# Gather stage of a two-layer graph kernel: four of a group's eight one-hot expansions moved from ScalarE to VectorE

## The reference

```python
weight = h @ (W_fc2 / 8.0)                # per edge, 4 x 32: wA, wC, wD, wB
g0, g1 = f0[edge_src], f1[edge_src]       # gathered rows, 32 and 32 x 3
e0, e1 = edge_attr[:, :1], edge_attr[:, 1:]
outA = wA * g0 * e0
outB = wB * einsum('euk,ek->eu', g1, e1) / SQRT3
outC = (wC * g0)[..., None] * e1[:, None, :]
outD = wD[..., None] * g1 * e0[..., None]
seg = lambda v: segment_sum(v, edge_dst)  # then scaled, mixed by small matrices, cos/sin, layernorm
```

## Time and profile before

| | us |
|---|---|
| median of 3 runs | 5282.36 (5281.97 to 5292.77) |
| the profiled execution | 5279.33 |
| its span, first to last instruction | 5277.7 |
| busy in the span: PE, VectorE, ScalarE, GpSimd | 3462.9, 2873.6, 2739.3, 4071.0 |
| gather stage, first to last gather instruction's start | 3262.97 to 5229.25 |

### The profile page before, as it was taken

How to read it: one execution, slowest core, us unless ns; L and a number is a source line. 1 busy time by engine, 2 the same in 40 slices (tenths; PEclk the granted TensorE clock), 3 DMA queues, 4 the chain that set the end, 5 groups by cost and what they waited for, 6 DMA issues and landing times. The chain is left out here.

```text
span 5277.7 us, 85398 instructions
## 1 busy us (share of the span) xinstructions
PE 3462.9 (66%) x18515; PEld 2879.1 (55%) x18515; DVE 2873.6 (54%) x12090; ACT 2739.3 (52%) x9367; POOL 4071.0 (77%) x3270
## 2 busy tenths in 40 slices
PE   3555555555555555555555376888888888888886
PEld 2334433344343443334333254878888888888886
DVE  5555556555556555565555366344454445444444
ACT  1222222222222222222222156899989998998997
POOL 2888888888888888888888764777777777777774
PEclk8777666666766666767676578777777777777777
DMA  8666666666666666666666595333333333333332
GB/s 278 114 114 109 117 110 114 114 115 113 108 114 114 115 115 113 111 110 115 115 114 113 82 245 153 85 89 91 91 89 89 90 91 89 89 92 90 88 90 63
DMA packets 704752, 587.38 MB, mean 111 GB/s; under 512 B 287387, under 2 KB 572624, under 8 KB 701623
## 3 DMA queue, kind: packets, MB, share of 16 engines
q0 software_dynamic: 285872, 224.40, 30.6%
q1 hardware_dynamic: 394090, 297.48, 20.0%
q10 hardware_dynamic: 24732, 64.87, 3.3%
HBM read 374.12 MB, written 212.29 MB: 111 GB/s over the span
## 5 line engine op out<-in xcount | busy, mean ns | idle before, releaser
L740 POOL DMA_INDIRECT sums_scratch<-vals,to_i x1564 | 2445.9, 1564 | 567.1 <-issue 385.8
L1069 POOL DMA_INDIRECT fg<-f_scratch,src_e x1564 | 1490.8, 953 | 497.9 <-issue 476.4
L646 PE MATMUL ps_n<-same,hot 128*40 128x128 f32 x3136 | 691.6, 413 | 1339.5 <-issue 1337.3
L1133 ACT ACTIVATE hot<-raw,e_s 128x40 f32<-128x40 f32 x6272 | 1390.9, 313 | 193.8 <-DVE raw L1250 151.3
L646 PEld LDWEIGHTS ps_n<-same,hot 128*40 128x40 f32 x3136 | 556.1, 184 | 1447.0 <-issue 1384.2
L689 ACT COPY near<-ps_n 40x512 f32<-40x512 f32 x196 | 113.3, 578 | 1677.7 <-PE ps_n L646 1677.7
L1098 PE MATMUL ps_eu<-hot,prod 128*128 128x120 f32 x3136 | 871.2, 371 | 0.0
L1096 PEld LDWEIGHTS ps_eu<-hot,prod 128*128 128x128 f32 x3136 | 612.1, 239 | 304.2 <-issue 267.2
L1096 PE MATMUL ps_eu<-hot,prod 128*128 128x40 f32 x3136 | 606.3, 284 | 256.1 <-issue 172.4
L1259 DVE TENSOR_TENSOR prod<-ps_ew,fg 128x256 f32<-128x256 f32 x392 | 164.6, 420 | 910.7 <-DMA fg<-f_scratch,src_e 905.6
L613 DVE TENSOR_TENSOR to_i<-away,srcf 128x8 int32<-128x8 f32 x196 | 32.9, 168 | 1123.3 <-POOLq L78 1123.2
(11 more groups left out here) (202 smaller groups left out, 4078.5 us busy)
## 6 DMA issues: line engine op xcount, KB each, us to landing
srow_s<-in_src SPq DMA_DIRECT2D x196, 512.0 KB
e_s<-in_edge_attr SPq DMA_DIRECT2D x196, 256.0 KB, 3.8
hid_scratch<-hid SPq DMA_DIRECT2D x196, 256.0 KB, 3.7
hid_e<-hid_scratch SPq DMA_DIRECT2D x196, 256.0 KB
sums_scratch<-zeros ACTq DMA_DIRECT2D x24, 1056.0 KB, 23.5
sums_scratch<-vals,to_i POOLq DMA_INDIRECT x1564, 3.4
fg<-f_scratch,src_e POOLq DMA_INDIRECT x1564
t_in<-sums_scratch POOLq DMA_DIRECT2D x72, 256.0 KB, 7.9
```

The costliest lines, as they stand in the source:

```text
L646: last = pe.matmul(ps_n[t // TH][:, t % TH, :], hot[:, k, t, :], same[:, k, t, :], start=True, stop=True)
L740: pool.indirect_dma_start(out=sums_d[i], out_offset=bass.IndirectOffsetOnAxis(ap=to_i[:, j, t:t + 1], axis=0), in_=vals[:, j, t, :], in_of ...
L1069: pool.indirect_dma_start(out=fg[:, j, t, :], out_offset=None, in_=f_d, in_offset=bass.IndirectOffsetOnAxis(ap=src_s[:, j, t:t + 1], axis= ...
L1133: last = act.activation(hot[:, k, t, c, :], raw[:, k, t, :], ACT.Copy, scale=e4_s[:, j, t, c:c + 1])
```

## The change

Of the eight tiles of a group, tiles 0 to 3 stay in ScalarE's 32 activations, of which 16 are left. Tiles 4 to 7 are written by one VectorE `tensor_tensor` of 128 x 640 (4 tiles x 4 attributes x 40), the product of `raw` and `e4_s`, both read from SBUF with broadcast dimensions. It stands between `raw` and `prod` of the same group. Before it VectorE waits for the attributes' load, for the segment matmuls of group `s-2` (`e_seg`) and for its own `raw`. A new semaphore `e_hot2` tells TensorE and SP that this half is ready or read.

```diff
@@ SP, before the loads of a group
                             done(sp, e_hot, s, UN)
+                            done(sp, e_hot2, s, UN)
                             done(sp, e_fc2, s, UN)
@@ TensorE, before the segment matmuls
                                 done(pe, e_hot, m)
+                                done(pe, e_hot2, m)
@@ ScalarE
-                                for t in range(TS):
+                                for t in range(TH):
                                     for c in range(4):
                                         last = act.activation(hot[:, k, t, c, :], raw[:, k, t, :], ACT.Copy,
                                                               scale=e4_s[:, j, t, c:c + 1])
@@ VectorE, between raw and prod
+                                uses(dve, e4_ld[j], q + 1, 16)
+                                done(dve, e_seg, s, 2)
+                                done(dve, e_raw, s)
+                                dve.tensor_tensor(hot[:, k, TH:TS, :, :], raw[:, k, TH:TS, None, :].to_broadcast([P, TH, 4, W]),
+                                                  e4_s[:, j, TH:TS, :, None].to_broadcast([P, TH, 4, W]), ALU.mult).then_inc(e_hot2, 1)
                                 done(dve, e_fc2, s)
```

More of the change, by code:

```diff
@@ L762, in graph_layers @@
         gath = [sem(f"e_gath{i}") for i in range(UN)]
-        e_fc2 = sem("e_fc2")
+        e_fc2, e_hot2 = sem("e_fc2"), sem("e_hot2")
         e_rel, e_raw, e_hot, e_prod = sem("e_rel"), sem("e_raw"), sem("e_hot"), sem("e_prod")
@@ L766, in graph_layers @@
         e_bases, clear_d = sem("e_bases"), sem("e_clear")
-        sems1 = src_ld + e4_ld + hid_ld + gath + [e_fc2, e_rel, e_raw, e_hot, e_prod,
+        sems1 = src_ld + e4_ld + hid_ld + gath + [e_fc2, e_hot2, e_rel, e_raw, e_hot, e_prod,
                                                   e_seg, e_sums, e_lin, e_add1, e_add, e_bases,
```

## The result

| | before, us | after, us |
|---|---|---|
| median, both kernels on one chip | 5281.96 (5277.62 to 5292.77, 10 runs) | 5295.14 (5289.20 to 5300.47, 10 runs) |
| ratio | | 1.0025 [1.0017, 1.0033] |
| the profiled execution | 5279.33 | 5300.47 |
| its span | 5277.7 | 5298.8 |
| first gather's start | 3262.98 | 3268.78 |

The kernel is slower by 13.2 us in the medians, a little over what can be told from no change. The profiled executions lie 21.1 us apart, and the lower rows split that: 5.8 us arise before the gather stage, in code that is the same in both kernels and therefore count as spread between two executions; 13.6 lie among the gathers; 1.7 come after them. The change owns the last two, 15.3 us.

A forecast was written before the change was run, and what follows sets the result against it. The prediction took GpSimd's back-to-back gathers as the bound. It summed 5279.33 us (profiled execution) + 13 for delayed gathers - 2 at the end to 5290.3, put the median at 5292, and gave a range of 5280 to 5313.

The forecast's parts named there:

- the likeliest case: Whole kernel: slower by +6 to +19 us over 5282.4, chance 0.60.
- The bound: Gather stage: GpSimd issues gathers back to back, 1.249 us each, and waits for nobody; ScalarE is busy beside the bound.
- ScalarE's relief at 0: Gather stage: removing 16 of 32 activations a group saves ScalarE 3.55 us of work, worth nothing for GpSimd's pace.
- The product's length: On VectorE, behind `raw`: one product of 128 x 640 takes 0.82 us.
- the two bounds: Product's length on VectorE: 0.75 us if the long row is cheaper, 1.3 if its broadcast ran at half rate beyond `raw`'s.
- Who is hit, and by how much: Gathers starting inside the two-SBUF-input product are late by its end minus their start minus 0.12 us, at most 0.65.
- The size, 13 us: Gather stage: delays from the product cost 13 us, between 8 from the trace's places and 33 with random starts.
- Not delaying `prod`: On VectorE: the product delays `prod` nowhere, as the least idle time before it is 1.7 us against 0.85.
- The added waits at 0: New waits of VectorE, SP and TensorE cost 0; cover gone, each at most up to 2.38 us.
- The end of the kernel, -2 us: After the last gather: ScalarE's relief lets the last `prod` start earlier, winning 2 us, between 0 and 3.6.

The follow-up runs named there:

- t0: Kernel before with ScalarE expanding tiles 0 and 7 only (8 activations of 32), segment sums using those two, no product: 5282.95 us, ratio 0.9988.
- t1: t0 plus the product behind `raw`, both inputs in SBUF, written to a spare tile nobody reads: 5305.12 us, ratio 1.0029 to the kernel before.
- t2: t1 with the product's second operand taken from PSUM, same shape: 5285.42 us, ratio 0.9994 to the kernel before.
- after_again: The changed kernel itself run again, against the kernel before on the same chip: 5297.62 us, ratio 1.0018.
- v3: Changed kernel with `rel` and the four tiles' attributes in PSUM, so `raw` and the product have one SBUF input each: 6355.34 us, ratio 1.0373 to before.
- e1b_relief: Kernel before with ScalarE expanding tiles 0 to 3 only, no product, tiles 4 to 7 summed with the first four's matrices: 6284.24 us, ratio 1.0250.

## Why the prediction was right, and where its working was not

The time was 5295.14 us, 3.1 above the forecast of 5292 and inside the likeliest case. That the mechanism was right is shown; that the number came so near is partly luck, since the gathers' 13 us rested on the wrong reason and the end had the wrong sign. Step by step:

- **The bound** was read rightly: gathers back to back, no wait. Of the views read, the busy shares of the earlier trace rows alone would have promised a gain.
- **ScalarE's relief at 0** for the pace: right, shown by t0.
- **The product's length**, 0.82 us: 0.825 measured, 0.824 to 0.827. Neither of the two bounds was needed; the upper one, 1.3, does not follow from its own words, which give 0.49 + 320 x 2.08 ns = 1.16.
- **Who is hit, and by how much**: right. The formula (end of the instruction - start of the gather - 0.12 us) fits the product as it did `raw`. The first half, "both inputs in SBUF is what hurts", was an inference from rows before, and t1 against t2 shows it. The Trainium skill's rule (SBUF — State Buffer, "Who interferes with whom") names the same pair of instructions, and the trace agrees; the time blocked is 0.12 us shorter at the end than the whole instruction, which the page gives.
- **The size, 13 us**: 13.7 of excess, but the step under it failed. The prediction set the product 0.03 us behind `raw`, as `raw` stands behind `rel`, and got 8 us; it then took 13 for fear that VectorE's place would move. The place did not move: x, the time from `raw`'s start to the next gather's, has medians of 0.05, 1.19, 0.20 and 0.50 us for the four j, where it had 0.05, 1.16, 0.20 and 0.48. The gap was mis-sized. It is 0.133 us in the median (4480.11 + 0.49 to 4480.73 is 0.13), so that the product ends 0.1 us later and each gather in it is held 0.1 us longer. The same reckoning behind the 195 `raw` of the trace before, with 0.13 in place of 0.03, hits 86 gathers by some 14.5 us, where 92 were hit by 15.3; with the 14.4 of before it gives about 29 us of excess, and 28.1 was measured. The right total came from a reserve taken for another reason.
- **Not delaying `prod`**: right in effect, too sure in its number. The least idle time left before `prod` was put at 1.7 - 0.85 us; it is 0.74 at 3503.11, and 0.30 in the last group, at 5251.27 in the rows below. VectorE's wait for rows fell from 877.9 to 702.2 us, by 176 (said: 160), and ScalarE's share is 56% (said: 56).
- **The added waits at 0**: right for all groups but one, where the product started 4.56 us after the end of `raw` (at 3269.72, the first group), in VectorE's own idle time.
- **The end of the kernel, -2 us**: wrong, +1.7. The step itself held: the last group's first `prod` came 2.6 us after the last gather's start, where it was 6.3. What it handed on to did not. The timeline of all engines at the end:

```profile
5248.69 0.95 POOL L1070 DMA_INDIRECT fg<-f_scratch,src_e  x1 [0.30 <-issue]
...
5251.27 0.42 DVE L1266 TENSOR_TENSOR prod<-ps_ew,fg 128x256 f32<-128x256 f32 x1 [0.30 <-DMA fg<-f_scratch,src_e]
...
5256.16 0.90 ACT L1143 COPY sums_a<-ps_eu 32x80 f32<-32x80 f32 x4 [2.46 <-PE ps_eu L1100]
...
5265.12 0.90 ACT L1143 COPY sums_a<-ps_eu 32x80 f32<-32x80 f32 x4 [7.62 <-PE ps_eu L1100]
```

ScalarE takes the last segment sums at 5265.12, 16.4 us behind the last gather's start at 5248.69. Before it did so 14.8 us behind 5229.25:

```profile
5244.01 0.90 ACT L1141 COPY sums_a<-ps_eu 32x80 f32<-32x80 f32 x4 [2.71 <-PE ps_eu L1098]
```

The windows of after around the last gather, columns as in the earlier trace rows:

```profile
5233.00:5241.00 8.00, 7.24 (x57) 6.68 (x57) 4.45 (x14) 2.39 (x11) 5.95 (x7) 1.00 0.24 66
5241.00:5254.00 13.00, 10.19 (x60) 9.50 (x59) 9.14 (x22) 9.88 (x39) 6.72 (x7) 0.80 0.22 62
5254.00:5263.00 9.00, 9.00 (x44) 9.00 (x44) 3.98 (x23) 1.29 (x5) 0.00 (x0) 0.50 0.00 0
```

and of before:

```profile
5222.00:5235.00 13.00, 13.00 (x54) 12.03 (x55) 4.48 (x13) 12.64 (x53) 6.36 (x7) 0.50 0.23 63
5235.00:5244.00 9.00, 8.99 (x79) 8.82 (x77) 6.28 (x26) 6.25 (x29) 0.00 (x0) 0.98 0.00 0
```

In 9 us around the last sums TensorE had its upper level (0.98 of 2.4 GHz) before and its lower one (0.50, 1.2 GHz) after, and did 44 matmuls where it did 79. The last group's segment matmuls began at

```profile
5240.17 0.39 PE L1096 MATMUL ps_eu<-hot,prod 128*128 128x40 f32 x2
```

before and at

```profile
5257.98 0.57 PE L1098 MATMUL ps_eu<-hot,prod 128*128 128x40 f32 x2
```

after, which is 10.9 and 9.3 us behind the last gather's start: 1.6 us were won. They took 3.8 us before and 7.1 after, and that makes of the gain the loss of 1.7; from ScalarE's copy to the end both kernels take 33.7 us. Ahead of the fall after, TensorE had been waiting twice for `prod`, 0.76 and 2.81 us (its timeline, up to 5248.94); before the same end it had been busy without a pause for 13 us, at the lower level. The level changes all through the stage (0.78 and 0.79 on average, in the earlier trace rows and its like after), so where it stands at the end may be chance. The fall repeats: in after_again the granted clock behind the last gather (5245.7) is the lower level again:

```profile
5246.00:5252.00 6.00, 6.00 (x29) 6.00 (x30) 5.18 (x15) 3.61 (x17) 0.63 (x1) 0.50 0.08 22
```

Its end took 50.0 us. That the pauses ahead bring the fall is argued from these traces, not tested.

## What to carry to other kernels

In this case GpSimd, which issues gathers back to back, was slowed by VectorE instructions with two SBUF inputs (`raw`, `t_sb`, the product) whenever a gather started in their hold, and by a plain copy in SBUF too (below). So work moved to VectorE is priced in GpSimd's time, not VectorE's: count the starts inside it, and the tail of the instruction after each. Where the product took one operand from PSUM, the cost went; where that needed a new wait (v3), the wait cost more on the chip where it ran. And before a reserve is added to an estimate, ask which term it stands for: here the gap was read behind an instruction of 0.17 us, and not behind one as long as `raw`.

## What the runs showed of the hardware

- The hold goes the other way as well, and is short: a `raw` in whose first 0.05 us a gather starts takes 0.52 to 0.57 us instead of 0.49, and that gather is not late (4472.94 above, with a gather at 4472.95).
- A VectorE instruction that depends on the one before it started 0.13 us behind `raw`, and 0.03 us behind `rel`, which is 0.17 us long. With its second operand in PSUM and a wait ahead it was 0.20 us.
- Two SBUF inputs are enough for the hold, but not needed. The copy of 128 x 512 from SBUF to SBUF (`staged`, one input, 0.43 us) holds gathers by the same formula. In t2_thin_psum 28 gathers started inside it and 9 were late, by 0.62 us together; in v3_both_psum 4, by 0.81. In before and after all starts inside it fell in its last 0.05 us, so these traces could not show it. A gather of t2_thin_psum, and VectorE's row from its own view: 0.34 - 0.12 = 0.22 us late.

```profile
3481.14 1.16 POOL L1071 DMA_INDIRECT fg<-f_scratch,src_e  x1 [0.30 <-issue]
```

```profile
3481.05 0.43 DVE L1292 COPY staged<-table 128x512 f32 x1 [0.24 <-DVE table L1286]
```

- The copy is also held by a gather: one that begins 0.63 to 0.75 us after a gather's start takes up to 0.57 us in after (23 of 49 over 0.44) instead of 0.43. Of 28 `raw` and 74 products at such a place in that trace none was longer.
- On three chips the same kernel took 5289, 6145 and 6134 us. In the traces of its variants on the slower two TensorE has pauses that the profile puts on issue (77 before `ps_ew` in 400 us of e1b_relief, up to 2.6 us), and the gathers are not the bound. There the product's half of the change was worth nothing and the other half 2.5 to 2.8%.
